# Rotation loop of a graph layer: the narrow counts last on TensorE, the first guess ahead of the count readers on VectorE

## What is computed

```python
def step(mat, t):                 # _build_mat, from the identity matrix
    i, j, theta = t
    c = jnp.cos(theta); s = jnp.sin(theta)
    ri = mat[i]; rj = mat[j]
    mat = mat.at[i].set(c * ri - s * rj)
    mat = mat.at[j].set(s * ri + c * rj)
    return (mat, None)
xn = _layernorm(x)
x = x + xn @ M + mix(xn)          # M = mat.T after a scan over (src, dst, edge_weight)
x = x + ffn(_layernorm(x))        # 8 experts, the best 2 of each row, exact gelu
```

## Time and profile before

| | |
|---|---|
| median of three runs | 1029.9 us |
| the profiled execution | 1028.55 us |
| its span, first to last instruction | 1026.7 us |
| TensorE busy | 939.8 us (92%) |
| VectorE busy | 725.3 us (71%) |
| ScalarE busy | 667.0 us (65%) |
| GpSimd busy | 593.5 us (58%) |
| mean granted TensorE clock | 0.969 |

### The profile page before, as it was taken

How to read it: one execution, slowest core, us unless ns; L and a number is a source line. 1 busy time by engine, 2 the same in 40 slices (tenths; PEclk the granted TensorE clock), 3 DMA queues, 4 the chain that set the end, 5 groups by cost and what they waited for, 6 DMA issues and landing times.

```text
span 1026.7 us, 26096 instructions
## 1 busy us (share of the span) xinstructions
PE 939.8 (92%) x6344; PEld 821.0 (80%) x6345; DVE 725.3 (71%) x2604; ACT 667.0 (65%) x1906; POOL 593.5 (58%) x927
## 2 busy tenths in 40 slices
PE   6899979899999999999998729999999989999997
PEld 4557758788888888888775419999989979999997
DVE  5965579789999889988768844444444447777775
ACT  6578747677777777776438736666656646666664
POOL 7813675566666566666426744666643246666664
PEclk8989999999999999999999959999999989999999
DMA  8323116611010000122115643444422223333332
GB/s 255 81 72 95 26 27 213 183 17 17 17 28 21 17 17 17 22 25 19 18 63 183 201 137 102 143 120 127 119 86 66 69 73 101 105 99 98 108 106 67
DMA packets 64684, 86.19 MB, mean 84 GB/s; under 512 B 18148, under 2 KB 52930, under 8 KB 64386
## 3 DMA queue, kind: packets, MB, share of 16 engines
q1 hardware_dynamic: 44879, 43.17, 15.2%
q0 software_dynamic: 19184, 42.04, 14.7%
q10 hardware_dynamic: 576, 0.54, 0.2%
HBM read 54.18 MB, written 33.02 MB: 85 GB/s over the span
## 4 chain that ended last, share of the span: by engine, by line
PE 55%; DVE 9%; issue 8%; DMA 5%; POOL 4%; ACT 3%; DVEq 1%; SPq 0%; POOLq 0%; ACTq 0%
PE banks L1920 16%; PE banks L1930 16%; PE banks L1744 5%; PE banks L1686 4%; PE banks L1755 4%; PE banks L1696 4%; DMA R<-incl_d,R 3%; POOL send_d L669 3%; PE banks L1911 2%; ACT R L759 2%; PE banks L1872 1%; PE banks L1727 1%; DVE R L1199 1%; DVE R L1172 1%; DVE Mrot L1254 1%
## 5 line engine op out<-in xcount | busy, mean ns | idle before, releaser
L1920 PE MATMUL banks<-R 128*128 128x128 f32 x1696 | 210.7, 278 | 2.4 <-ACT R L995 2.4
L1920 PEld LDWEIGHTS banks<-R 128*128 128x128 f32 x1696 | 201.5, 195 | 3.0 <-ACT R L995 2.9
L1930 PE MATMUL banks<-R 128*128 x848 | 201.4, 381 | 0.0
L1008 ACT ACTIVATE R<-banks,b1c 128x128 f32<-128x128 f32 x424 | 143.3, 365 | 52.4 <-PE banks L1920 50.6
L1930 PEld LDWEIGHTS banks<-R 128*128 128x128 f32 x848 | 153.9, 191 | 16.7
L995 ACT ACTIVATE R<-banks,bet_c,gam_c 128x128 f32<-128x128 f32 x212 | 85.6, 454 | 106.0 <-PE banks L1911 102.4
L1526 DVE COPY R<-R 128x1024 f32 x106 | 74.1, 700 | 76.7 <-PE banks L1920 60.8
L669 POOL DMA_INDIRECT send_d<-R,slot_all x98 | 95.9, 979 | 50.7 <-issue 42.8
L682 POOL DMA_INDIRECT first_d<-R,dest_now x54 | 58.9, 1090 | 96.9 <-DVE R L1531 87.7
L1744 PEld LDWEIGHTS banks<-R 128*128 128x128 f32 x768 | 95.6, 191 | 17.3 <-ACT R L891 15.7
L1744 PE MATMUL banks<-R 128*128 128x126 f32 (+5 forms) x768 | 104.3, 279 | 4.6 <-ACT R L891 4.6
(11 more groups left out here) (323 smaller groups left out, 1922.9 us busy)
## 6 DMA issues: line engine op xcount, KB each, us to landing
R<-send_d SPq DMA_DIRECT2D x106, 131.0 KB
R<-in_L_ffn_W_dram SPq DMA_DIRECT2D x16, 512.0 KB
R<-in_x_dram SPq DMA_DIRECT2D x14, 512.0 KB, 4.8
R<-in_x_dram SPq DMA_DIRECT2D x5, 1024.0 KB, 11.0
rec_d<-R SPq DMA_DIRECT2D x1, 2800.0 KB
send_d<-zrow SPq DMA_DIRECT2D x14, 131.0 KB, 5.9
send_d<-R,slot_all POOLq DMA_INDIRECT x98
R<-incl_d,R POOLq DMA_INDIRECT x80
```

The source lines that it names most:

```text
L1008: last = nc.scalar.activation(hT[b][:, c, :], bank[2 + 2 * b + c // 2][:, (c % 2) * P:(c % 2 + 1) * P], ACT.Gelu, bias=b1c[:, bass.ds(e, 1 ...
L1920: last = mm(bank[2 + 2 * b + c // 2][:, (c % 2) * P:(c % 2 + 1) * P], w1c[b][:, kb, c * P:(c + 1) * P], xmT[b][:, kb * P:(kb + 1) * P], st ...
L1930: last = mm(bank[6 + b][:, 0:D], hT[b][:, c, :], w2s[:, bass.ds(e, 1), c, :].rearrange("p a h -> p (a h)"), start=(c == 0), stop=(c == H / ...
```

## The change

Two places of the hand-written order differ, and nothing else. On TensorE the two sorts of narrow counts move from before `turn_L` to behind `better` of level 5, the end of a turn. On VectorE `first_guess` of the next group moves from behind `kept` to ahead of `find_last` and `kept`, the two operations that read the counts. The wait for `D_done`, the last thing that `kept` does, is then the last thing in the turn.

```diff
                 factor(k, 5)
                 rows_read(k)
+                first_guess(k1)
                 find_last(k1)
                 kept(k)
-                first_guess(k1)
...
                 residual(k, 5)
+                turn_L(k + 1)
+                better(k, 5)
                 count_writes(k)
                 count_later(k + 1)
-                turn_L(k + 1)
-                better(k, 5)
```

## The result

The changed kernel takes 1034.96 us (median of 17 runs), the kernel before beside it 1029.9 us (17 runs): ratio 1.0059, 95% interval 1.0048 to 1.0069. It is slower by 5 to 7 us. The profiled execution spans 1032.8 us, against 1026.7.

What follows compares the result with a forecast made beforehand. VectorE's stream across the turn's boundary was taken to bound the kernel. Ten steps of 0.40 us plus 0.3 at the exit gave +4.3 us on 1029.9, forecast 1034.2 us, range 1029.5 to 1037.5.

Steps and rivals of the forecast that it cites:

- what bounds the turn: VectorE's stream across the turn's boundary sets when TensorE may go on; what is added there is added to the turn.
- the mechanism: VectorE's loop end: nothing covers the branch and register steps behind the D_done wait, so swap's copies start 0.40 us later.
- The value taken, 0.40: VectorE's delay per step, between 0.31 and 0.46 us because the trace doesn't show which form the wait takes.
- the long turns: Five of 15 steps, where ScalarE waits for gathered rows, are free: a boundary delay under 0.51 us only shortens that wait.
- its sign: Ordinary turns between transforms on TensorE would be 21.99 us (21.90 to 22.05) in the profile after.
- The rival in which all 15 pay: Late rows come later along with the delay: 15 x 0.40 + 0.3 = 6.3 us, 1036.2 us; chance 0.15.
- the exit: After the loop, the same wait and branch make TensorE's L1798 0.2 to 0.4 us later; 0.3 taken.
- The sum: Ten paying steps at 0.40 us plus 0.3 at the exit: +4.3 us; bounds of the step give 3.3 to 5.0.
- a hidden branch: VectorE's stream passes the loop's branch while kept is under way: no difference, 1029.9 us; chance 0.12.
- a free wait: VectorE needs no time between kept and what waits for it: 1.9 us saved, 1028.0 us; chance 0.08.
- TensorE late: Counts at TensorE's stream end delay its branch, moving transform by 0.1 to 0.2 us; at worst 1036.2 us; chance 0.05.

Runs made afterwards that it cites:

- the two parts alone: Kernel before with only VectorE's part of the change: turn 22.22 us, ratio 1.0056; with only TensorE's part: turn 21.59 us, ratio 0.9995.
- the one with the gather later: Changed kernel plus two useless small GpSimd operations ahead of gather L576, which moved it by 0.12 us: turn 21.95 us, ratio 1.0036 to the kernel before.

## Why the prediction was right, and where it was short

**Right: what bounds the turn.** VectorE's stream across the boundary set the time; the two parts alone show it, with 22.22 and 21.59 us.

**Right: the mechanism.** The loop's own steps were covered by `first_guess` and are covered by nothing afterwards. The wait moved past the branch takes the loss away with no other change. The copies come 0.32 us later by the timeline (2.42 less 2.10); the bounds were 0.31 and 0.46. The lower one was worked out for a wait that rides on the loop's own register step, as it rode on L311, and that is the form it took. The value taken, 0.40, lay between the forms and was 0.08 us too high.

**Short: the length of what follows.** The turn grew by 0.61, not 0.40. The sum took the copies and `take_fields` at the durations of the trace before. But they moved by 0.32 us against GpSimd, whose gather starts at its old place: 2.52 us after `rows_read` in both kernels. The prediction used just this (the gather doesn't follow the boundary) to free the long turns, and didn't ask what the moved operations would meet. The one slow copy of 0.25 us in the trace before could have raised the question. `take_fields` lost 0.22 us there, `swap`'s copies 0.07 (0.51 for five instead of 0.44). 0.32 + 0.22 + 0.07 = 0.61. So the turn lies outside the 21.90 to 22.05 us that the prediction gave as its sign. The experiments show the 0.22 from both sides. The 0.07 is one copy of the five. L1224 in this turn, first the changed kernel, then the one with the gather later (count, duration in ns as min/median/max, first and last start):

```profile
L1224 DVE COPY R<-R x5: 156/157/217, 353.2 to 353.6; 128x4 f32<-128x4 f32 x5
```

```profile
L1227 DVE COPY R<-R x5: 155/165/191, 350.0 to 350.3; 128x4 f32<-128x4 f32 x5
```

In the changed kernel the long one is the second, which starts at 353.29, 0.02 us ahead of the gather at 353.31. With the gather 0.12 us later the long one is the fourth, at 350.24, 0.01 us behind the gather at 350.23. In the kernel before, where the five have started before the gather, none takes more than 0.166 us. The long copy moves with the gather.

**Right: the long turns are nearly free, shown for three of the five.** Rows of the changed kernel, ScalarE's timeline, the last three turns:

```profile
450.93 0.46 ACT L768 ACTIVATE R<-R,sought_in 128x200 f32<-128x200 f32 x1 [0.89 <-DMA R<-incl_d,R]
...
473.26 0.46 ACT L768 ACTIVATE R<-R,sought_in 128x200 f32<-128x200 f32 x1 [1.02 <-DMA R<-incl_d,R]
...
496.01 0.46 ACT L768 ACTIVATE R<-R,sought_in 128x200 f32<-128x200 f32 x1 [1.53 <-DMA R<-incl_d,R]
```

The first wait was 1.48 and the three together 5.2; now they are 3.4. What VectorE adds, this wait gives back. TensorE's timeline, first the kernel before, then the changed one, `transform` at the start of the ten ordinary turns, at their end, and at the end of the last three:

```profile
215.75 2.05 PE L1727 MATMUL banks<-R 128*128 128x128 f32 x16 [0.38 <-ACT R L891]
...
431.68 2.05 PE L1727 MATMUL banks<-R 128*128 128x128 f32 x16 [0.38 <-ACT R L891]
...
498.73 2.05 PE L1727 MATMUL banks<-R 128*128 128x128 f32 x16 [0.38 <-ACT R L891]
```

```profile
218.91 2.05 PE L1727 MATMUL banks<-R 128*128 128x128 f32 x16 [0.33 <-DVE R L1249]
...
440.94 2.05 PE L1727 MATMUL banks<-R 128*128 128x128 f32 x16 [0.33 <-DVE R L1249]
...
508.15 2.05 PE L1727 MATMUL banks<-R 128*128 128x128 f32 x16 [0.33 <-DVE R L1249]
```

Ten turns: 215.93 and 222.03 us, +6.10, ten times 0.61. The last three: 67.05 and 67.21, +0.16, for 0.61 is a little more than the 0.51 that the shortest of them had to spare. The rival in which all 15 pay would have given 9.2 us with 0.61 a step, and falls by these three.

**Too high: the exit.** It was put at 0.3 us and is 0.08: by TensorE's timeline L1798 starts 2.11 us after the last `transform` (510.26 less 508.15), 2.03 before (500.76 less 498.73). VectorE's scaling L1321 starts 1.29 us after that `transform` instead of 1.21, so it came only 0.08 later. Why it is so little was not tested.

**The sum.** 6.10 + 0.16 + 0.08 = 6.3 us, beside 4.3 predicted; the first two long turns together went from 46.59 to 46.12 us, and over all profiles of this case they ranged from 44 to 50, so by their length they say nothing of 0.6 us (ScalarE's two waits for rows in them fell from 5.3 to 3.6 us, which fits free turns). The ratio's interval says 4.9 to 7.1, the medians 5.06. The forecast was right in direction and in the mechanism of the larger part, and low by the collision, which no rival contained. That 1034.2 lies only 0.8 us from the median is in part luck: the changed turns cost 6.3 us, above the 3.3 to 5.0 that the bounds of the step gave. The overestimate of the steps (0.08 a turn) hid part of the missing 0.29, and the medians differ by less than the turns do. The rivals of a hidden branch and of a free wait fall with the changed kernel's own turn. TensorE late falls with its part alone.

**Not settled.** The spans differ by 6.1 us, but that this is near the 6.3 of the turns is chance. The changed kernel's profiled execution was already 3.6 us later at the first `first_guess` (149.9, against 146.3), in work that the change doesn't touch. It was 9.5 us later at L1798, and took 3.4 us less from there to the end. Single executions scatter that much outside the loop, so turns, not spans, carry the argument here. What moves this part from run to run wasn't looked into.

## What to carry to other kernels

An operation in front of a loop's branch can hide the branch, the register steps and the waits of the next turn's head, if it is long enough (0.69 us was, here) and nothing between it and the branch waits for a result. A wait for an engine's own short result belongs behind the branch, as near as possible to whoever reads the result. And after working out by how much operations move, look again at what they now stand beside on the engine whose timing doesn't move: here 0.29 of the 0.61 us a turn, nearly half of the loss, were such meetings.

## What the runs showed of the hardware

- A 24-element copy by VectorE took 0.40 us instead of 0.18 when it began 0.60 us after the start of a 1.03 us gather by GpSimd, and ended 0.03 us before the gather. Beginning 0.11, 0.22 or 0.46 us after the start it was not touched. A 4-element copy that began within 0.02 us of the gather's start took 0.19 to 0.22 us instead of 0.16. A sum over an axis of length one, of the same 24 numbers at the same place, was not touched at 0.60 us either, and took 0.18 us.
- VectorE's loop steps, from the end of the wait on the first register step to the first operation of the next turn, took 0.39 us (352.82 to 353.21) with nothing beside them, and added nothing under an operation of 0.69 us.
- The narrow products on TensorE start 0.025 us apart (twelve in 0.3 us), and their place in the stream made no difference to a turn.
